# Latent transposes of the next sequence in bank m1 beside the key scores instead of in bank m2 beside the turned pair

## The reference

```python
xn = _layernorm(x, axis=-1)
x = x + _L0_attn_ref(xn, Wq, Wkv_down, Wk_up, Wv_up, Wo) + _L0_ffn_ref(xn, w_gate, w_up, w_down)

# attention
q = (x @ Wq.T).reshape(b, t, N_HEADS, HEAD_DIM)
kv_latent = x @ Wkv_down.T                      # 64 numbers per token
k = (kv_latent @ Wk_up.T).reshape(...)
v = (kv_latent @ Wv_up.T).reshape(...)
attn = softmax(einsum('bqhd,bkhd->bhqk', q, k) * HEAD_DIM ** -0.5)
out = einsum('bhqk,bkhd->bqhd', attn, v).reshape(b, t, N_HEADS * HEAD_DIM) @ Wo.T

# feed-forward, every operand rounded to FP4 in blocks of 16
h = silu(fp4_linear(x, w_gate)) * fp4_linear(x, w_up)
y = fp4_linear(h, w_down)
```

## Time and profile before

| | |
|---|---|
| runs | 1688.26, 1689.79, 1696.55 us; median 1689.79 us |
| profiled execution | 1696.03 us, of which the span is 1694.0 us |
| mean granted TensorE clock | 0.974 of full speed |
| PE busy | 1577.0 us, 93% of the span |
| DVE busy | 1340.1 us, 79% |
| ACT, POOL busy | 708.9 us (42%), 517.8 us (31%) |

### The profile page before, as it was taken

One profiled execution on the slowest core, in us unless ns is written; L12 is line 12 of the kernel. 1 busy time (PEld: TensorE's weight loads), 2 busy tenths in 40 slices (PEclk: granted clock), 3 DMA queues, 4 the chain that ended last, 5 costly groups with the idle time before them and its releaser, 6 DMA issues.

```text
span 1694.0 us, 30412 instructions
## 1 busy us (share of the span) xinstructions
PE 1577.0 (93%) x10726; PEld 1442.1 (85%) x10726; DVE 1340.1 (79%) x3368; ACT 708.9 (42%) x1382; POOL 517.8 (31%) x696
## 2 busy tenths in 40 slices
PE   0599999999999999999999999999999999999998
PEld 0488998989889898988989899898989989898897
DVE  8788787888888888888878788878888877787663
ACT  2444444444444444444443444444344444344432
POOL 7433232332232233323223323223233322332211
PEclk9799999999999999999999999999999999999999
DMA  3000000000000000000000000000000000000000
GB/s 98 7 10 4 8 20 4 19 8 11 14 8 17 7 20 7 10 14 7 17 7 20 4 14 14 8 17 7 20 5 14 14 4 20 7 11 8 1 14 13
DMA packets 22885, 22.60 MB, mean 13 GB/s; under 512 B 3280, under 2 KB 22224, under 8 KB 22736
## 3 DMA queue, kind: packets, MB, share of 16 engines
q1 hardware_dynamic: 22736, 20.65, 4.0%
HBM read 11.99 MB, written 8.39 MB: 12 GB/s over the span
## 4 chain that ended last, share of the span: by engine, by line
PE 87%; DVE 9%; issue 3%; ACT 1%; DMA 0%; POOL 0%; SPq 0%; DVEq 0%; POOLq 0%
PE m L774 35%; PE po L904 23%; PE mx L863 7%; PE st L889 7%; PE st L890 6%; PE m L876 3%; PE m L1010 2%; PE m L1016 1%; PE m L928 1%; DVE row_max L611 1%; PE m L1024 1%; DVE hid L595 1%; DVE on_lo L745 1%; DVE h_small L583 1%; DVE x_small L583 1%
## 5 line engine op out<-in xcount | busy, mean ns | idle before, releaser
L904 PEld LDWEIGHTS po<-lat_tok,probs 128*128 128x128 f32 x4096 | 523.5, 194 | 22.9
L904 PE MATMUL po<-lat_tok,probs 128*128 128x65 f32 x4096 | 519.1, 270 | 0.0
L506 ACT ACTIVATE probs<-st 128x512 f32<-128x512 f32 x512 | 291.3, 595 | 338.2 <-PE st L890 338.2
L611 DVE TENSOR_REDUCE row_max<-mx 128x1 f32<-128x512 f32 x512 | 327.7, 682 | 0.6 <-PE mx L863 0.6
L411 POOL TENSOR_TENSOR h_norm<-hid,h_small 128x352 f32<-128x352 f32 x128 | 100.8, 788 | 480.7 <-DVE h_small L588 480.7
L889 PE MATMUL st<-q_hi,lat 128*128 128x512 f32 x512 | 212.7, 415 | 0.0
L890 PE MATMUL st<-q_lo,lat 65*128 65x512 f32 x512 | 203.6, 398 | 0.0
L774 PE MATMUL m<-wgu_hi,xt_hi 128*128 128x352 f32 x512 | 191.9, 375 | 0.1
L724 DVE TENSOR_TENSOR q_lo<-m,q_hi 64x512 fp32r<-64x512 f32 x128 | 88.1, 688 | 122.4 <-ACT q_hi L546 122.4
L442 POOL TENSOR_TENSOR h_norm<-h_norm,hid 128x352 f32<-128x352 f32 x128 | 119.7, 935 | 211.6 <-DVE h_norm L597 211.6
L863 PE MATMUL mx<-lat,q_hi 128*128 128x512 f32 x512 | 176.5, 426 | 4.0 <-DVE row_max L611 3.9
(11 more groups left out here) (178 smaller groups left out, 3054.2 us busy)
## 6 DMA issues: line engine op xcount, KB each, us to landing
x_in<-in_L_attn_x_dram SPq DMA_DIRECT2D x64, 128.0 KB, 2.2
out_dram<-acc SPq DMA_DIRECT2D x32, 256.0 KB, 2.3
q_lo<-neg_max SPq DMA_DIRECT2D x128, 2.0 KB
weights_in<-in_L_ffn_w_down_dram SPq DMA_DIRECT2D x1, 704.0 KB, 6.3
weights_in<-in_L_ffn_w_gate_dram SPq DMA_DIRECT2D x1, 640.0 KB, 4.7
acc<-in_L_ffn_w_up_dram SPq DMA_DIRECT2D x1, 640.0 KB, 5.9
wq_in<-in_L_attn_Wq_dram SPq DMA_DIRECT2D x1, 512.0 KB, 5.9
x_in<-in_L_attn_Wo_dram SPq DMA_DIRECT2D x1, 512.0 KB, 7.0
```

Of the source, the lines that this page charges most:

```text
L506: act.activation(probs[:, t.c % 2, kc, :], st[kc % 2][:, :], ACT.Exp).then_inc(exp_done, 1)
L611: dve.tensor_reduce(row_max[:, u.c % 2, qc:qc + 1], mx[qc % 2][:, :], AX.X, ALU.max).then_inc(mx_taken, 1)
L904: last = pe.matmul(po[:, qc * P:qc * P + R + 1], probs[:, u.c % 2, kc, qc * P:(qc + 1) * P], lat_tok[:, s.c % 2, kc, 0:R + 1], start=(kc = ...
```

## The change

In slot 6 of each 8 the four transposes of the next sequence's latents are issued earlier, just after key scores 2 and 3, and write m1 instead of m2. They wait for the latents (lat_lo_done) and for the last reader of the up projection in m1 (hid_done), and no longer for on_lo_done. Their two readers, on ACT and DVE, read m1. The up projection of slot 7 now waits for ltok_done, since it writes m1 next; the row maxima of slot 7 now wait for on_lo_done, since the turned pair is now the last in m2.

```diff
@@ ACT
-                    act.activation(lat_tok[:, s.c % 2, :, 0:R], m2[:, :].rearrange("p (c r) -> p c r", c=CH)[:, :, 0:R],
+                    act.activation(lat_tok[:, s.c % 2, :, 0:R], m1[:, :].rearrange("p (c r) -> p c r", c=CH)[:, :, 0:R],
@@ DVE
-                    dve.tensor_tensor(whole, m2[:, :].rearrange("p (c r) -> p c r", c=CH)[:, :, R:P], whole,
+                    dve.tensor_tensor(whole, m1[:, :].rearrange("p (c r) -> p c r", c=CH)[:, :, R:P], whole,
@@ def m1_free(t)
+                elif ltok_seq(t) is not None:
+                    pe.wait_ge(ltok_done, ltok_seq(t).n(1, 1))
@@ def m2_free(t)
-                elif ltok_seq(t) is not None:
-                    pe.wait_ge(ltok_done, ltok_seq(t).n(1, 1))
@@ PE slot, after key_scores(t, 2) and key_scores(t, 3)
-                if s is not None or q_pair(t) is not None:
+                if s is not None or q_pair(t) is not None or ltok_seq(t) is not None:
...
+                s = ltok_seq(t)
+                if s is not None:
+
+                    pe.wait_ge(lat_lo_done, s.n(1, 1))
+                    for c in range(CH):
+                        last = pe.transpose(m1[:, c * P:(c + 1) * P], lat[:, s.c % 2, c * P:(c + 1) * P].bitcast(F32), ident[:, :])
+                    last.then_inc(ltok_psum, 1)
@@ PE slot, before weigh(t, 3)
-                if s is not None:
-
-                    if m is not None:
-                        pe.wait_ge(on_lo_done, m.n(1, 1))
-                    pe.wait_ge(lat_lo_done, s.n(1, 1))
-                    for c in range(CH):
-                        last = pe.transpose(m2[:, c * P:(c + 1) * P], lat[:, s.c % 2, c * P:(c + 1) * P].bitcast(F32), ident[:, :])
-                    last.then_inc(ltok_psum, 1)
```

More of the change, by code:

```diff
@@ L994, in slot @@
                 m = turned_pair(t)
-                s = ltok_seq(t)
-                if n is not None or m is not None or s is not None:
+                if n is not None or m is not None:
                     if t.plus(-2).within(SLOTS):
```

## The result

The changed kernel takes 1637.22 us (median of 4 runs, 1636.45 to 1639.45), the kernel before 1690.66 us in the same comparison: ratio 0.9683, 95% interval 0.9664 to 0.9701. The forecast was 1641.6 us with a range from 1635 to 1657. The profiled execution of the changed kernel took 1636.52 us, 59.5 us less than that of before.

What follows compares the result with a forecast made beforehand. TensorE, busy 93% of the span, was taken as the bound. 1696.0 - 34.6 (stops) - 20.8 (clock falls) + 1.0 (up projection) = 1641.6 us; range 1635 to 1657.

Steps and rivals of the forecast that it cites:

- The stop: TensorE's wait for on_lo at the latent transposes goes: 2.31 us at each of 15 places, 34.6 us.
- The moved transposes don't wait: Latent transposes in their new place in slot 6 find latents and hid_done ready: cost 0.
- Row maxima: Slot 7's new wait for on_lo doesn't bite: 0.5 us of room, cost 0.
- Up projection: Slot 7's new wait for lat_tok is tight: 0.09 us of room, 1 us taken for all 15.
- DVE's lag in slot 7: Silu starts about 1.4 us behind the row maxima, leaving 0.7 us of room at the down projection: cost 0.
- The clock: Falls of TensorE's granted clock behind the stops at the latent transposes vanish: 20.8 us.
- The first rival: The stop at the latent transposes goes but the clock falls stay: 1656 us for the median, chance 0.11.

Runs made afterwards that it cites:

- the run with lat_tok late: Changed kernel with DVE's half of lat_tok moved behind the rounding of the next tokens: 1660.7 us, ratio 0.9818 to the kernel before.
- putting the stop back: Changed kernel with slot 6's last probability products also waiting for ltok_done: 1684.9 us, ratio 0.9962 to the kernel before.
- the run with the stop behind the up projection: Changed kernel with key scores 0 in slot 7 also waiting until DVE has taken query scores 1 (mx_taken): 1685.9 us, ratio 0.9972.
- the run with stops between wide products: Changed kernel with slot 7's up projection also waiting for silu_done, ahead of products of 352 and 512 columns: 1666.7 us, ratio 0.9844.
- the run with medium stops beside thin work: Changed kernel with slot 6's last probability products (65 columns, near transposes) also waiting for on_lo_done: 1680.9 us, ratio 0.9925.
- the short stop: Changed kernel with slot 6's last probability products also waiting for on_hi_done: 1650.8 us, ratio 0.9757 to the kernel before.

## Why the prediction was right

- *The stop.* Forecast: 6.40 us become 4.09. Measured: 4.03, so 2.37 us each. The prediction counted 15 equal stops, but the last is 0.7 us shorter (1.41 us printed), so they come to 34.8 us, against 34.6 forecast: the two deviations nearly cancel, which is luck. The four transposes took 0.43 us (741.07 to 741.50, where the products follow) instead of 0.50; the first transpose behind a stop lasts 328 ns against 272.
- *The moved transposes don't wait.* Shown by the list of waits.
- *Row maxima.* on_lo ended at 744.58, PE came at 745.10: 0.5 us of room, as computed.
- *Up projection.* The estimate was 0.09 us of room and 1 us of cost, the measured room is 0.2 us and the cost 0. DVE started lat_tok 0.60 us behind on_lo, not 0.73 as between the two works of slot 4. That the place is tight was shown by the run with lat_tok late.
- *DVE's lag in slot 7.* Forecast: silu 1.4 us behind the row maxima, and 0.7 us of room at the down projection. Measured: 746.40 against 745.10, so 1.3; ht_lo ends at 748.58 us and the down projection starts at 749.69, so 1.1 us of room, and the list of waits has no entry there.
- *The clock.* Forecast: no falls, 20.8 us. No fall was left in the profiled execution. What they had cost is what the two profiled executions leave: 59.5 - 34.8 (stops) - 1.7 (lead, next point) = 23.0 us. A second way gives the same: the first and the last latent transposes are 1403.8 us apart before and 1350.1 after, 53.7 less, of which 32.5 are the stops between them; with 1.6 for the fall behind the last that makes 22.8. That the stops bring them is shown by putting the stop back. The first rival, falls without a stop, is ruled out by the same trace and by the run with only the bank changed.
- *What the sum did not hold.* The row maxima of slot 0 came at 99.34 us before and at 97.62 after. It isn't the change that gave these 1.7 us. One wait of 0.63 us in the lead went with it (82.47 us, row maxima for lat_tok), but the query scores ahead of that place came 1.85 us earlier in the changed kernel (76.89 against 78.74) and those behind it 1.84 (82.82 against 84.66). The two clock levels fall differently in the lead, as in the stretch from 70 to 80 us with a mean of 0.67 before and 0.82 after; that this is the whole of it is argued, not shown. Before:

```profile
99.34 0.28 PE L928 MATMUL m<-ident,row_max 128*4 128x128 f32 x1
```

after:

```profile
97.62 0.28 PE L928 MATMUL m<-ident,row_max 128*4 128x128 f32 x1
```

With 0.2 (stops), 1.0 (up projection), 1.7 (lead) and 2.2 (falls) the difference from 1641.6 to the profiled 1636.5 us is made up. It closes by construction, since the falls were taken as the remainder; the second way above is the check on it.

Two readings need a word. The prediction says that TensorE stood still for 2.1 us at each fall; at the last, at 1571 us, it was 1.4. And from all falls standing beside thin work I took, for the run with the stop behind the up projection, that a fall needs it. The kernel before had no stop near 2 us elsewhere, so its trace could not have told, and the one fall of the run with stops between wide products speaks against it, if weakly, since three transposes follow 1.5 us behind that stop.

## What to carry to other kernels

When an engine that bounds the kernel waits for a bank that two readers must clear, look for a bank whose last reader is long done at that point; here that alone was worth 3.1%, and the place in the queue nothing. Price a stop of TensorE by the starts around it and by the time of like work behind it, not by its idle time: here 31.2 us of printed idle time cost 57.8 in the profiled execution (34.8 for the stops, 23.0 for the clock). Then list the waits again: 42 of 0.4 us that looked like noise gave another 24 us for one transpose moved between products that need nothing from it.

## What the runs showed of the hardware

- Between 150 and 1600 us the granted clock fell to 1.2 GHz behind stops of 1.4 to 2.2 us printed, at 1 to 13 of 15 places in a run, and never behind the 42 stops of 0.4, 15 of 0.7 or 14 of 1.5 us. So no length divides them: 1.4 us beside thin work brought a fall in the kernel before (1571 us) and in the run with medium stops beside thin work (1557 us; granted clock 0.56 from 1558 to 1561.4), 1.5 us ahead of wide products none. A full fall cost 2.9 us in the kernel before, and some 5 us with the stop behind the up projection.
- A stop of 1.4 us with one of 1.3 close behind it brought a fall too, but not always: in the runs with the short stop and with lat_tok late the same two left the clock at 1.00. In the tail of the changed kernel two stops of 1.4 and 1.3 us are followed by a stretch at 0.50:

```profile
1618.03 0.55 PE L876 MATMUL m<-ident,hq 128*128 128x128 f32 x3 [1.41 <-DVE on_lo L745]
1619.85 0.55 PE L774 MATMUL m<-wd_hi,ht_hi 128*128 128x256 f32 x1 [1.26 <-DVE ht_lo L657]
```

```profile
1620.00:1625.00 5.00, 4.49 (x20) 4.19 (x21) 0.42 (x1) 0.00 (x0) 0.00 (x0) 0.50 0.00 0
```

- With stops of the same 1.7 us, falls stood at 8 of 15 places beside transposes and products of 65 columns, and at 1 of 15 between products of 352 and 512 columns (with the one transpose of the row maxima just ahead of the stop, and the next ones 1.5 us behind it).
- Which of several equal stops is followed by a fall differs: 9 of 15 in the kernel before, 13 of 15 after only the row maxima were moved, with the stops nearly unchanged. What decides it stays open.
- A run of eight transposes of 128 x 128 without a stop left the clock at 1.00 from 150 to 1600 us (the run with only the bank changed).
